# The output projection of grouped attention: from twelve split matmuls a step to four unsplit ones in full precision

## The reference

```python
q = (h @ Wq).reshape(B, S, NH, HD)
k = (h @ Wk).reshape(B, S, KVH, HD)
v = (h @ Wv).reshape(B, S, KVH, HD)
q = _rope(q, pos)
k = _rope(k, pos)
...
scores = jnp.einsum('bqhd,bkhd->bhqk', q, k) / jnp.sqrt(jnp.float32(HD))
causal = jnp.tril(jnp.ones((S, S), dtype=bool))
scores = jnp.where(causal[None, None], scores, jnp.float32(-1000000000.0))
attn = jax.nn.softmax(scores, axis=-1)
o = jnp.einsum('bhqk,bkhd->bqhd', attn, v).reshape(B, S, NH * HD) @ Wo
x = resid + o
```

## Time and profile before

| | |
|---|---|
| median of 3 runs | 1761.63 us (1759.51 to 1761.83) |
| the profiled execution, its own time | 1762.68 us |
| span of the profiled execution | 1760.9 us |
| PE busy over the span | 1432.3 us (81%) |
| DVE busy | 1015.7 us (58%) |
| ACT busy | 706.4 us (40%) |
| POOL busy | 613.7 us (35%) |

### The profile page before, as it was taken

The page is one execution under the profiler, slowest core; times in us unless marked ns, Lnnn a source line. Parts: engine busy times, 40 slices in busy tenths (PEclk is TensorE's granted clock), DMA queues, the critical chain, the costliest instruction groups (busy, mean ns, idle before and its releaser), DMA issues. The chain is left out here.

```text
span 1760.9 us, 24199 instructions
## 1 busy us (share of the span) xinstructions
PE 1432.3 (81%) x8658; PEld 1035.9 (59%) x8690; DVE 1015.7 (58%) x1651; ACT 706.4 (40%) x1386; POOL 613.7 (35%) x549
## 2 busy tenths in 40 slices
PE   4886498879868457988678888888889968999997
PEld 3653343654368344443455666666667646888886
DVE  4763655427865447775656666676666654343343
ACT  2552200316522314666244554454444523444442
POOL 4100100000054342110645555555555433555552
PEclk8998655869989677889889999999999987999998
DMA  1000000020000010000200000000000012332331
GB/s 62 2 1 16 25 0 25 25 94 0 0 0 0 1 33 1 2 2 1 73 7 7 25 13 13 19 19 13 13 19 13 13 37 75 122 104 104 116 114 45
DMA packets 28668, 55.27 MB, mean 31 GB/s; under 512 B 5295, under 2 KB 16495, under 8 KB 28448
## 3 DMA queue, kind: packets, MB, share of 16 engines
q1 hardware_dynamic: 28576, 54.05, 9.4%
HBM read 51.67 MB, written 2.27 MB: 31 GB/s over the span
## 5 line engine op out<-in xcount | busy, mean ns | idle before, releaser
L1626 POOL TENSOR_TENSOR a_o_low<-a_o,a_o_high 128x512 fp32r<-128x512 f32 x64 | 83.2, 1299 | 172.4 <-ACT a_o_high L1923 172.4
L2322 DVE TENSOR_TENSOR e_act<-e_gated,ps 128x512 f32<-128x512 f32 x66 | 45.4, 688 | 165.2 <-POOL e_gated L2172 165.2
L2015 DVE TENSOR_REDUCE a_nmax<-ps 128x2 f32<-128x512 f32 x64 | 44.3, 692 | 165.8 <-PE ps L1746 165.8
L1617 POOL TENSOR_TENSOR a_raw<-a_prod 128x512 f32<-128x512 f32 x72 | 93.5, 1298 | 86.9 <-DVE a_prod L2008 86.9
L1923 ACT ACTIVATE a_o_high<-a_o 128x512 fp32r<-128x512 f32 x64 | 40.4, 631 | 207.3 <-PE ps L1678 198.6
L1897 ACT ACTIVATE a_shift<-ident,a_nmax 128x128 bf16<-128x128 f32 x256 | 81.9, 390 | 70.7 <-DVE a_nmax L2017 70.6
L2172 POOL TENSOR_TENSOR e_gated<-e_gate,e_wb 128x512 f32<-128x512 f32 x66 | 85.1, 1291 | 56.3 <-ACT e_gate L2255 44.9
L1678 PE MATMUL ps<-a_h_high,a_wq_high 128*128 128x512 f32 x128 | 58.3, 455 | 52.9 <-DVE a_prod L2008 51.3
L2163 POOL TENSOR_TENSOR e_we_low<-e_we,e_we_high 128x768 fp32r<-128x768 f32 x33 | 60.8, 1841 | 93.1 <-ACT e_we_high L2260 93.1
L575 DVE TENSOR_REDUCE x_nmax<-ps 128x2 bf16<-128x512 f32 x128 | 82.6, 691 | 11.6 <-PE ps L349 11.1
L1420 DVE SCALAR_TENSOR_TENSOR m_acc<-ps,m_conv_w,m_acc 128x1020 f32<-128x1020 f32 (+2 forms) x60 | 76.2, 1275 | 20.6 <-ACT m_acc L1365 19.2
(11 more groups left out here) (420 smaller groups left out, 4406.2 us busy)
## 6 DMA issues: line engine op xcount, KB each, us to landing
e_wb<-token_weights SPq DMA_DIRECT2D x33, 512.0 KB, 4.0
e_we<-in_experts SPq DMA_DIRECT2D x33, 384.0 KB, 3.1
a_wq<-in_a_wq SPq DMA_DIRECT2D x16, 256.0 KB, 3.0
a_wo<-in_a_wo SPq DMA_DIRECT2D x16, 256.0 KB, 2.8
m_win<-in_m_winT SPq DMA_DIRECT2D x1, 3080.0 KB
nf_raw<-in_ffn_w SPq DMA_DIRECT2D x3, 352.0 KB
ffn_deq<-nf_wout SPq DMA_DIRECT2D x3, 352.0 KB
x<-in_x SPq DMA_DIRECT2D x1, 1024.0 KB
```

Of the source, the lines that this page charges most:

```text
L1617: e.tensor_tensor(raw[:, i % 2, :], prod[:, i % 2, 0, :], prod[:, i % 2, 1, :], ALU.add).then_inc(s_raw, 1)
L1626: e.tensor_tensor(oL[:, s % 3, :], o[:, s % 2, :], oH[:, s % 3, :].bitcast(F32), ALU.subtract).then_inc(s_ol, 1)
```

## The change

The projection takes `o` and `Wo` as they are. The twelve fp32r matmuls of a step, 256 columns each, become four float32 matmuls of 256 columns. The functions `wo_high`, `wo_low`, `o_high` and `o_low` go, with their buffers and semaphores. `divide` writes `o` into a ring of four buffers (`o_ring`) in place of two, and waits for the projection four steps back (`s_out`) in place of the low part two steps back (`s_ol`). `project` waits for the DMA of `Wo` (`s_wo`), for `divide` (`s_o`) and, as before, for the residual addition (`s_add`). The order of the calls on each engine is otherwise unchanged.

```diff
@@ -1604,10 +1604,6 @@
-        def wo_low(e, p):
-            e.wait_ge(s_woh, p + 1)
-            e.tensor_tensor(woL[:, p % 2], wo[:, p % 2], woH[:, p % 2].bitcast(F32), ALU.subtract).then_inc(s_wol, 1)
...
-        def o_low(e, s):
-            e.wait_ge(s_oh, s + 1)
-            e.tensor_tensor(oL[:, s % 3, :], o[:, s % 2, :], oH[:, s % 3, :].bitcast(F32),
-                            ALU.subtract).then_inc(s_ol, 1)
@@ -1651,18 +1642,13 @@
-            wo_low(e, 0)
             wq_low(e, 1)
             for n in range(N + PD):
-                if 0 <= n - PD < N:
-                    o_low(e, n - PD)
...
-                if c == 1 and 1 <= p - 1 < NP:
-                    wo_low(e, p - 1)
@@ -1810,15 +1796,15 @@
             def project(s):
                 p = s // B
-                e.wait_ge(s_wol, p + 1)
-                e.wait_ge(s_ol, s + 1)
+                e.wait_ge(s_wo[p % 2], 16 * (p // 2 + 1))
+                e.wait_ge(s_o, s + 1)
                 if s >= 1:
                     e.wait_ge(s_add, s)
                 for t in range(2):
                     at = lambda j: slice(j * S + t * P, j * S + (t + 1) * P)
-                    mm = three(ps[:, OUT, t * D:(t + 1) * D],
-                               [(oH[:, s % 3, at(j)], oL[:, s % 3, at(j)], woH[:, p % 2, j, :], woL[:, p % 2, j, :])
-                                for j in range(2)])
+                    for j in range(2):
+                        mm = e.matmul(ps[:, OUT, t * D:(t + 1) * D], oR[:, s % 4, at(j)], wo[:, p % 2, j, :],
+                                      start=(j == 0), stop=(j == 1))
                 mm.then_inc(s_out, 1)
@@ -1866,10 +1852,6 @@
-            def wo_high(p):
-                e.wait_ge(s_wo[p % 2], 16 * (p // 2 + 1))
-                e.activation(woH[:, p % 2], wo[:, p % 2], ACT.Copy).then_inc(s_woh, 1)
@@ -1915,12 +1897,6 @@
-            def o_high(s):
-                e.wait_ge(s_o, s + 1)
-                if s >= 3:
-                    e.wait_ge(s_out, s - 2)
-                e.activation(oH[:, s % 3, :], o[:, s % 2, :], ACT.Copy).then_inc(s_oh, 1)
@@ -1943,11 +1919,8 @@
-            wo_high(0)
             wq_high(1)
             for n in range(N + PD):
-                if 0 <= n - PD < N:
-                    o_high(n - PD)
...
-                if c == 0 and 1 <= p - 1 < NP:
-                    wo_high(p - 1)
@@ -2034,9 +2005,9 @@
             def divide(s):
                 e.wait_ge(s_over, s + 1)
                 e.wait_ge(s_av, s + 1)
-                if s >= 2:
-                    e.wait_ge(s_ol, s - 1)
-                e.tensor_tensor(o[:, s % 2, :], ps[:, AV, :], over[:, s % 2, :], ALU.mult).then_inc(s_o, 1)
+                if s >= 4:
+                    e.wait_ge(s_out, s - 3)
+                e.tensor_tensor(oR[:, s % 4, :], ps[:, AV, :], over[:, s % 2, :], ALU.mult).then_inc(s_o, 1)
```

More of the change, by code:

```diff
@@ L1524, in stage_attention_1 @@
         wq, wqH = sb("wq", [P, 2, 2, KD, P]), sb("wq_high", [P, 2, 2, KD, P], F32R)
-        wo, woH = sb("wo", [P, 2, 2, D]), sb("wo_high", [P, 2, 2, D], F32R)
+        wo = sb("wo", [P, 2, 2, D])
         wkL, wvL = sb("wk_low", [P, KD, NKV * P], F32R), sb("wv_low", [P, KD, NKV * P], F32R)
-        wqL, woL = sb("wq_low", [P, 2, 2, KD, P], F32R), sb("wo_low", [P, 2, 2, D], F32R)
+        wqL = sb("wq_low", [P, 2, 2, KD, P], F32R)
         rot = sb("rot", [P, 4, S])
@@ L1541, in stage_attention_1 @@
         inv, invH, invS = sb("inv", [P, 2, S]), sb("inv_high", [P, 2, S], F32R), sb("inv_split", [P, 2, S], F32R)
-        oH, oL = sb("o_high", [P, 3, 2 * S], F32R), sb("o_low", [P, 3, 2 * S], F32R)
+        oR = sb("o_ring", [P, 4, 2 * S])
         s_wk, s_wv, s_rot, s_mask, s_pick = (sem(n) for n in ("wk_in", "wv_in", "rot_in", "mask_in", "pick_in"))
@@ L1546, in stage_attention_1 @@
         s_wq, s_wo = [sem(f"wq_in_{i}") for i in range(2)], [sem(f"wo_in_{i}") for i in range(2)]
-        s_wqh, s_wql, s_woh, s_wol = sem("wq_high"), sem("wq_low"), sem("wo_high"), sem("wo_low")
+        s_wqh, s_wql = sem("wq_high"), sem("wq_low")
         s_wch, s_wcl = sem("wk_wv_high"), sem("wk_wv_low")
@@ L1558, in stage_attention_1 @@
         s_bc, s_over = sem("inverses_spread"), sem("inverses_copied")
-        s_av, s_o, s_oh, s_ol = (sem(n) for n in ("values_summed", "o_ready", "o_high", "o_low"))
+        s_av, s_o = sem("values_summed"), sem("o_ready")
         s_out, s_add = sem("projected"), sem("added")
```

## The result

| | before | after |
|---|---|---|
| median | 1761.73 us (4 runs, 1759.51 to 1762.74) | 1784.18 us (4 runs, 1783.20 to 1786.89) |
| ratio, 95% interval | | 1.0128 (1.0113 to 1.0143) |
| span of the profiled execution | 1760.9 us | 1782.1 us |

The change makes the kernel 1.3% slower. The forecast was 1781.5 us, with a range of 1774 to 1791. A second set of four runs of the changed kernel, beside experiments, gave 1783.43 us (1779.58 to 1784.21) and a ratio of 1.0138 (1.0121 to 1.0155) to the kernel before beside it, 1759.48 us.

The account below looks back on a forecast made before the run. The prediction took the loop as bound by a ring of waits between PE and DVE, with the projection uncovered. 1762.68 + 21.1 (projection) - 1.3 (start) = 1782.5; the median stands 1.05 lower, so 1781.5 us, range 1774 to 1791.

Parts of the forecast that it names:

- The ring: In the attention loop PE and DVE wait for each other: first scores, maxima, rotation, piece, projection, first scores; projection uncovered.
- The projection's price: Projection on PE, between piece and first scores: 1.73 us in place of 1.40, +0.33 a step, +21.1 us over 64 steps.
- ACT's and POOL's work at nothing: Removed splitting on ACT and POOL, about 124 us of engine time, costed at nothing on the path except at loop start.
- counting the tail in full: The eleven last projections, with no piece beside them, lengthen the path too, so all 64 projections were counted.
- The start: At the loop's start, without a_wo_high and a_wo_low ahead, the first piece starts earlier: -1.3 us, between 0 and -1.6.
- The clock: PE's clock in two-piece steps: lowered around two of six, at most 1.7 us each; change taken as 0, -3.4 to +6.8.
- New waits: DVE's divide waits for the projection four steps back, and project waits for Wo's DMA; both cost 0.
- two passes, not four: Rival: each new projection matmul takes 0.215 us, the projection 0.86 in place of 1.40; 1725.7 us in all; chance 0.03.
- Absorbed: Rival: PE's 58.5 us of waiting for the rotation take up the longer projection, leaving only -1.3; 1760.3 us; chance 0.04.
- DVE freed: Rival: DVE's split is on the ring and 32 fall from 1.018 to 0.483 us, -17.1; 1764.4 us; chance 0.03.
- Dearer: Rival: float32 weight loads or changeovers show in each step, projection 1.95 us, +14 us more; 1795.6 us; chance 0.06.

Follow-up runs that it names:

- e2: Kernel before with only the high x high products in the projection, four matmuls a step in place of twelve; 1708.49 us, ratio 0.9708.
- e3: Kernel before with the projection moved ahead of the pieces in PE's step and DVE's residual addition one step earlier; 1718.63 us, ratio 0.9750.
- e4: Changed kernel with the projection moved ahead of the pieces in PE's step and DVE's residual addition one step earlier; 1733.10 us, ratio 0.9830.
- e1: Changed kernel with the removed splitting work put back on ACT and POOL, results unused; 1780.20 us, ratio 1.0098 to the kernel before.
- e7: Kernel before with the high and low parts of Wq made ahead of those of Wo at the loop's start; 1763.36 us, ratio 1.0017.
- e5: Kernel before with the projection moved ahead of the piece, or between the two pieces where a step has two; 1709.00 us, ratio 0.9719.
- e6: Changed kernel with the projection moved ahead of the piece, or between the two pieces where a step has two; 1718.65 us, ratio 0.9778.

## Why the prediction was right, and one term of it wrong

- **The ring** was right in each link: PE's waits for a_prod did not change (58.4 us), DVE's for first scores grew by 22.0, and both kinds of step grew by 0.33 us. The experiments show it from both sides: a projection shorter by 0.93 us shortens every step by as much (e2), and one that stands elsewhere is free in the odd step (e3, e4).
- **The projection's price**, +0.33 a step, was measured at 0.33 (8.48 to 8.81, 7.86 to 8.19). The row that had priced it, the unsplit matmul of the same stage at 0.86 us for 512 columns, was the right one; the 1.78 of the group in the first attention contained its changeover. Over steps 7 to 63 the sum is +19.0, and with 2.5 in the tail 21.5, where +21.1 was forecast; the surplus is about what the two lowered steps among these cost more than before (13.7 against 13.17).
- **ACT's and POOL's work at nothing**: right (e1). So was counting the tail in full.
- **The start, "-1.3 us, between 0 and -1.6"**: this is the step that failed. The piece does start 1.2 us earlier after its first scores, with 0.36 us of waiting in place of 1.58; this is PE in the changed kernel:

```profile
883.64 0.77 PE L1664 MATMUL ps<-a_h_high,a_wq_high 128*128 128x512 f32 x1 [0.36 <-POOL a_wq_low L1605]
```

  But the first seven steps together take 50.65 us in place of 50.01. Of the 1.2 gained, 0.4 went in the second step (5.89 in place of 5.47), where the clock stood at a mean of 0.88 in place of 1.00; the prediction had named this way of losing it. The rest was lost because the first two-piece step fell to the low level (11.90 in place of 10.36), as in every trace with the new order. The term was +0.6 in this trace, outside its range, and the same edit alone is 0.17% slower (e7). The prediction had the clock as an error on both sides of 0 and the start as a sure gain. They are not independent, since the start shifts the steps.
- **The clock**: "at most 1.7 us" a step was 1.4 to 1.7 in these two kernels (11.73 to 13.17, 10.36 to 11.90, 12.07 to 13.7). Three of six two-piece steps were low in place of two. That steps 7 to 63 had two low ones before and after, so that this term came out near the 0 that was taken, is luck: other traces with the same wait of 2.22 us had one to five of them.
- **New waits**: neither `divide` nor the DMA of `Wo` shows one, as said.
- The time came out 2.7 us above the forecast; 1.9 of it are the start term's wrong sign (+0.6 in place of -1.3), as far as one trace tells.
- **The rivals**: *two passes, not four* is out, as a matmul has two records 0.215 us apart and the group takes 1.71. *Absorbed* is out where the projection stands, and true in the odd step where e4 puts it: the place decides. *DVE freed* is out: the split's mean fell only from 0.970 to 0.929 us in the loop and its median stayed (1.018 and 1.015). With POOL's work put back (e1) the mean is 0.933, so even that small gain does not hang on POOL's subtractions. And the split runs behind the rotation, where DVE waits anyway. *Dearer* is out: it asked for 0.55 us a step and 0.33 came.

## What to carry to other kernels

Where two engines wait for each other in turn, work counts by where it stands. Between the last thing that one engine waits for and the first that the other waits for, it is paid in full; in front of a wait it is free up to the length of that wait. So look for the engine's longest wait and put the longest movable work ahead of it, before counting passes. Taking work from engines that only wait was worth nothing here, and even a shorter start lost, by shifting which steps lost the clock.

## What was not expected

PE's clock in the two-piece steps. With the wait of 2.22 us for a rotation it falls in some of them and not in others: 1 to 5 of 6 in the eight traces that keep this wait in all six. The stretch of 10 us around one of them in the changed kernel and a stretch around one that kept its clock (columns as in rows 1):

```profile
960.00:970.00 10.00, 7.77 (x29) 5.45 (x27) 5.70 (x10) 3.14 (x8) 3.83 (x3) 0.83 0.01 3
...
1110.00:1120.00 10.00, 8.18 (x52) 5.74 (x52) 6.10 (x9) 2.12 (x7) 2.47 (x2) 1.00 0.10 28
```

A lowered step costs 1.3 to 1.7 us over the traces, so this alone moves the kernel by up to 0.5%. With the wait cut to 0.86 us (e5) or 0.50 (e6) it did not occur in ten steps.

There is one more place where the clock falls, which the prediction did not count. Step 3 (the steps are counted from 0) has one piece, and PE waits 3.14 us for its rotation. In the kernel before it reads

```profile
900.13:908.64 8.51, 5.37 (x24) 4.03 (x23) 5.09 (x7) 2.96 (x8) 3.01 (x3) 0.80 0.00 0
```

and in e1 and e3 the same step keeps a clock of 1.00 and takes 7.08 us. That is most of why their first seven steps take 49.04 us, against 50.01 here.

The start of the loop can also be seen to shift it: the order of two 0.6 us copies and two 1.3 us subtractions ahead of a loop of 64 steps changed the time by 0.17%, against its local effect (e7).
